# Second layer of a gated attention and expert network on one core: sums of expert rows, norm and rotary attention as one program, loads spread over beats

## What is computed

```python
x = x + tanh(g_xattn[0]) * L0_xattn(_layernorm(x), ctx)   # self-attention with a mask, LN, cross-attention, LN, feed-forward, LN
x = x + tanh(g_ffn[0])   * L0_ffn(_layernorm(x))          # 8 experts, top 2, FF = 1024
x = x + tanh(g_xattn[1]) * L1_xattn(_layernorm(x), ctx, mask)   # rotary cross-attention
x = x + tanh(g_ffn[1])   * L1_ffn(_layernorm(x))          # 8 experts, top 1

# L1_xattn
q = larope(heads(x @ Wq + bq), Lq); k = larope(heads(ctx @ Wk + bk), Lk); v = heads(ctx @ Wv + bv)
scores = where(mask, q @ k.T * 64 ** -0.5, -inf)
return softmax(scores) @ v @ Wo + bo
# L0_ffn
out = out + combine[:, e:e + 1] * (relu(xt @ W1[e] + b1[e]) @ W2[e] + b2[e])   # over the experts e
```

## Time and profile before

| what | value |
| --- | --- |
| median of three runs | 1515.91 us (1514.93 to 1516.16) |
| profiled execution: its time, its span | 1511.45 us, 1509.7 us |
| mean granted clock of PE | 0.917 |
| PE busy in the span | 1216.6 us (81%) |
| DVE / ACT / POOL busy | 749.2 / 565.3 / 419.6 us |
| DMA, mean over the span | 108 GB/s |

### The profile page before, as it was taken

The page is one execution under the profiler, slowest core; times in us unless marked ns, Lnnn a source line. Parts: engine busy times, 40 slices in busy tenths (PEclk is TensorE's granted clock), DMA queues, the critical chain, the costliest instruction groups (busy, mean ns, idle before and its releaser), DMA issues. The chain is left out here.

```text
span 1509.7 us, 27319 instructions
## 1 busy us (share of the span) xinstructions
PE 1216.6 (81%) x8458; PEld 980.7 (65%) x8513; DVE 749.2 (50%) x2742; ACT 565.3 (37%) x1353; POOL 419.6 (28%) x736
## 2 busy tenths in 40 slices
PE   3699989999985999889999996047987865499991
PEld 2466666666653888788888895035665535399991
DVE  3587767676752567743322221846876832122212
ACT  1265656565652322233333332012654541133330
POOL 2434544434334244310000001642334121410004
PEclk9799999999997999999999998567998985699996
DMA  8675676565621920111111112635453204472103
GB/s 216 137 162 149 148 201 151 145 142 147 139 84 52 376 86 36 40 56 36 36 33 35 34 36 90 169 74 106 96 108 72 55 10 153 163 256 90 38 32 118
DMA packets 128612, 162.47 MB, mean 108 GB/s; under 512 B 15444, under 2 KB 113372, under 8 KB 123612
## 3 DMA queue, kind: packets, MB, share of 16 engines
q1 hardware_dynamic: 120072, 133.67, 33.6%
q0 software_dynamic: 8416, 27.27, 5.2%
HBM read 103.23 MB, written 55.19 MB: 105 GB/s over the span
## 5 line engine op out<-in xcount | busy, mean ns | idle before, releaser
L820 DVE CUSTOM_DVE_ANT_0 att_masked_scores<-att_S,Bm 128x256 bf16<-128x256 f32 x512 | 191.6, 419 | 57.4 <-PE att_S L518 46.1
L662 ACT ACTIVATE att_PT<-att_T 128x512 f32<-128x512 f32 x256 | 151.6, 595 | 86.2 <-PE att_T L538 77.1
L1721 ACT ACTIVATE moe_hT<-moe_H,moe_b 128x128 f32<-128x128 f32 x312 | 89.3, 369 | 192.1 <-PE moe_H L1634 191.5
L1987 POOL DMA_INDIRECT comb_g<-yd,dest x48 | 45.7, 952 | 407.1 <-PEq L1971 391.9
L1634 PEld LDWEIGHTS moe_H<-moe_aT,ff_w 128*128 128x128 f32 x1248 | 145.1, 192 | 8.8 <-DVE ff_w L1919 6.2
L1634 PE MATMUL moe_H<-moe_aT,ff_w 128*128 128x128 f32 x1248 | 146.1, 275 | 5.5 <-DVE ff_w L1919 4.9
L1646 PE MATMUL moe_Z<-moe_W,moe_hT 128*128 x624 | 142.5, 381 | 0.8 <-DVE moe_z L1926 0.8
L1646 PEld LDWEIGHTS moe_Z<-moe_W,moe_hT 128*128 128x128 f32 x624 | 115.4, 190 | 15.5 <-issue 1.2
L518 PE MATMUL att_S<-L_KS,L_QS 96*128 96x256 bf16 x512 | 99.2, 276 | 19.5 <-DMA L_KS<-att_k_dram 10.4
L1926 DVE TENSOR_TENSOR moe_z<-moe_Z,moe_b 128x256 f32<-128x256 f32 x39 | 16.6, 424 | 195.5 <-PE moe_Z L1646 195.5
L538 PE MATMUL att_T<-L_QS,L_KS 99*128 99x256 bf16 x512 | 98.4, 273 | 5.3 <-issue 2.6
(11 more groups left out here) (422 smaller groups left out, 2249.4 us busy)
## 6 DMA issues: line engine op xcount, KB each, us to landing
xd<-zero SPq DMA_DIRECT2D x14, 1280.0 KB
moe_W<-in_L_ffn_W SPq DMA_DIRECT2D x16, 1024.0 KB, 13.4
...
att_q_dram<-att_pq SPq DMA_DIRECT2D x16, 384.0 KB, 4.3
att_k_dram<-att_pk SPq DMA_DIRECT2D x16, 384.0 KB, 2.6
L_QS<-att_q_dram SPq DMA_DIRECT2D x16, 384.0 KB, 4.8
L_KS<-att_k_dram SPq DMA_DIRECT2D x16, 384.0 KB, 7.8
...
```

The source lines that it names most:

```text
L662: nc.scalar.activation(PT[:, h % 8, :], bankT[h % 2][:, :], ACT.Exp).then_inc(exp_done, 1)
L820: ins = nc.vector.tensor_tensor_reduce(masked_scores[:, h % 2, u, :], bankS[h % 2][:, u * SEQ:(u + 1) * SEQ], masks[m // B][0][:, u * SEQ: ...
L1721: ins = nc.scalar.activation(eT[:, s % 2, g * P:(g + 1) * P], bankH[half][:, f * P:(f + 1) * P], ACT.Relu, bias=b1[:, bass.ds(e * NF + g, 1)])
```

## The change

- `prepare` loads only what it uses, and rows 0 and 1. The stack rows, rows 2 to 7 and `OUTER` of layer one are issued by SP in beats -4 to -1 of `att`, the context in beat 1, the weights of layer two (ten loads) in beat 2 (`load_in_beats`).
- In `TASKS` and in all engines' loops, rows are turned (and copied by ACT) at head 10 and the output product is made (and added by DVE) at head 12; before it was the other way round.
- `combine` in front of the rotary attention is gone, and `attention_pipeline` has lost its rotary branches. `rotary_pipeline` does both: POOL issues four gathers of 128 expert rows per sequence (`gather`), DVE adds them (`sum_experts`, `sum_rows`) and makes the moments, POOL the roots (`input_roots`, in place of ACT's square root), DVE the norm (`input_norm`).
- In it, keys and values of sequences 0 and 1 are made ahead of the beats, before the first rows are normed; the beats start at -3. SP waits for the spread of queries and of keys by semaphores of their own. V is filled with ones by DVE, not by POOL.
- The instructions of one head, one projection, one split into parts are the same as before.

```diff
@@ prepare, sync
-            rows(0)
+            load_rows(sp, mem, X, a["x"], 0)
...
-            rows(1)
-            load_stack_rows(sp, mem, a["c_stack_rows"])
-            for n in range(2, B):
-                rows(n)
-            load_weights(sp, mem, 0, OUTER)
-            load_weights(sp, mem, 1, INNER + OUTER)
-            load_context(sp, mem)
+            load_rows(sp, mem, X, a["x"], 1)
@@
-         10: (("z", -1),), 11: (("o", 1),), 12: (("x", 4),), 14: (("c", 4),), 15: (("o", 2),)}
+         10: (("x", 4),), 11: (("o", 1),), 12: (("z", -1),), 14: (("c", 4),), 15: (("o", 2),)}
@@
+def load_in_beats(sp, mem, X, x, stack_rows, b):
+    if b == -4:
+        load_stack_rows(sp, mem, stack_rows)
+        load_rows(sp, mem, X, x, 2)
+    if -4 <= b < -1:
+        load_rows(sp, mem, X, x, b + 7)
+    if b == -2:
+        load_rows(sp, mem, X, x, 6)
+        load_weights(sp, mem, 0, OUTER)
+    if b == -1:
+        load_rows(sp, mem, X, x, 7)
+    if b == 1:
+        load_context(sp, mem)
+    if b == 2:
+        load_weights(sp, mem, 1, INNER + OUTER)
@@ attention_pipeline, sync
                     max_to_queries(b + 1)
...
+                load_in_beats(sp, mem, X, *loads, b)
@@ attention_pipeline, tensor (scalar and vector alike)
-                    if h == 10 and has(b - 1):
+                    if h == 10 and has(b + 4):
+                        turn_rows(b + 4)
+                    if h == 12 and has(b - 1):
                         project_out(b - 1)
-                    if h == 12 and has(b + 4):
-                        turn_rows(b + 4)
@@ rotary_pipeline, sync
+            load_rotary(sp, mem)
+            spread_parts(0, 1)
+            stack(0, 1)
+            for b in BEATS:
+                if 3 <= b + 2 < M:
+                    stack(b + 2, 0)
+                    stack(b + 2, 1)
+                if b == -1:
+                    max_to_queries(0)
+                if has(b + 3):
+                    spread_parts(b + 3, 0)
+                    if b + 3 < 3:
+                        stack(b + 3, 0)
+                if b == -3:
+                    load_rest(sp, mem)
+                    spread_parts(1, 1)
+                    stack(1, 1)
+                if b >= 0 and has(b + 1):
+                    max_to_queries(b + 1)
+                if AHEAD <= b + 3 < M:
+                    spread_parts(b + 3, 1)
+                    if b + 3 < 3:
+                        stack(b + 3, 1)
@@ rotary_pipeline, tensor
+            for m in range(AHEAD):
+                turn_context(m)
+                keys(m)
+                project_values(m)
+            turn_rows(0)
@@ rotary_pipeline, scalar
+            bring_context(0)
+            first_part(0, 1)
+            second_part(0, 1)
+            bring_context(1)
+            bring_rows(0)
@@ rotary_pipeline, gpsimd
+            gather(0)
+            gather(1)
+            input_roots(0)
+            parts(0, 1)
+            for b in BEATS:
+                if has(b + 4) and b != -2:
+                    input_roots(b + 4)
+                if has(b + 3):
+                    parts(b + 3, 0)
+                if b == -2:
+                    input_roots(2)
+                if has(b - 2):
+                    inverse_roots(nc, pool, t, moments, root_step, b - 2).then_inc(rooted, 1)
+                if b == -3:
+                    gather(2)
+                    parts(1, 1)
+                if AHEAD <= b + 3 < M:
+                    parts(b + 3, 1)
+                if has(b + 6):
+                    gather(b + 6)
@@ rotary_pipeline, vector
+            def sum_experts(n, i):
+                dve.wait_ge(gathered[n % RING], 16 * NU * TOP * (n // RING + 1))
+                for u in range(NU):
+                    at = n * NU + u
+                    if i:
+                        dve.wait_ge(summed, NU * (TOP * n + 1))
+                    nc.vector.scalar_tensor_tensor(X[:, at, :], g[:, n % RING, i, u, :], weight[i][:, at:at + 1], X[:, at, :],
+                                                   ALU.mult, ALU.add).then_inc(summed, 1)
...
+            nc.vector.memset(V[:, :, :, :], 1.0).then_inc(ready0, 1)
+            dve.wait_ge(mem["k_in"], 16 * 4)
+            turned_keys(0)
+            dve.wait_ge(mem["v_in"], 16 * 3)
...
+            value_rows(0)
+            sum_rows(0)
+            input_moments(0)
+            sum_rows(1)
+            input_norm(0)
+            input_moments(1)
+            turned_keys(1)
+            value_rows(1)
...
+                    if h == 1 and b == -2:
+                        sum_rows(2)
+                        input_moments(2)
+                        sum_rows(3)
+                    if h == (9 if b == -2 else 2) and has(b + 4):
+                        input_norm(b + 4)
...
+                    if h == 5 and b >= -1 and has(b + 5):
+                        sum_experts(b + 5, 0)
+                    if h == 6 and b >= -1 and has(b + 5):
+                        sum_experts(b + 5, 1)
...
+                    if h == 14 and b >= -2 and has(b + 5):
+                        input_moments(b + 5)
@@ flamingo
-            combine(nc, "comb0", X, Y, 2, yd0, dest, weight, mem=mem, stack_rows=a["c_stack_rows"])
-            attention_pipeline(nc, "out", c, mem, X, Y, lambda m: True, gate=gate_x1)
+            rotary_pipeline(nc, "out", c, mem, X, Y, gate_x1, yd0, dest, weight)
```

730 lines of the change are left out of this document (560 added, 170 removed).

## The result

| what | before | changed |
| --- | --- | --- |
| median, beside one another on one chip | 1515.42 us | 1488.91 us (1487.47 to 1490.82) |
| ratio, 95% interval | | 0.9831 [0.9809, 0.9853] |
| span of the profiled execution | 1509.7 us | 1486.2 us |
| mean granted clock of PE | 0.917 | 0.915 |

What follows compares the result with a forecast made beforehand. PE was taken to set the pace in attention, with nobody working between stages. Terms -9.0 - 17.2 + 1.5 - 13.1 + 7.6 gave -30.2 us: 1481.3 us profiled, 1485.7 us against the median, range 1475 to 1501.

Steps and rivals of the forecast that it cites:

- A: Kernel start: loads taken out of the preparation let the first attention start earlier; -9.0 us, bounds -10 and -6.5.
- B: First attention's beats: rows turned at head 10, output product at head 12, so PE's wait goes; -17.2 us.
- Rival 2: First attention: the add at head 12 still waits for `ybb`, all of B is lost; 1502.9 us, chance 0.15.
- C: First attention: loads moved into its beats lengthen them; +1.5 us, bounds 0 and +5.
- D: Rotary start: sums, norm and first keys inside the rotary program bring transposed scores earlier; -13.1 us, bounds -18 and -4.
- Rival 3: Rotary start: held by POOL's queue, so D gives 4 us instead of 13; 1494.8 us, chance 0.1.
- Rival 4: Rotary start: D better than its sum, loads landing at 945 and added DVE work finding gaps; 1478 us, chance 0.1.
- E: Rotary beats 0 to 3: added sums, moments and norms, and late data in beat 0; +7.6 us, bounds +3 and +12.
- Rival 1: Rotary beats -1 to 2: DVE and POOL block one another at sums and norm; 14.4 us, 1500.1 us, chance 0.15.
- Rival 5: Rotary beats -1 to 2: idle gaps drop PE to its lower clock; four such beats give 1570 us, chance 0.02.

Runs made afterwards that it cites:

- experiment 1: Kernel before with only rows turned at head 10 and output product at head 12, in both attention programs: 1494.44 us against 1513.73, ratio 0.9868.
- experiment 2: Kernel before with only the loads moved out of the preparation into the beats: 1512.5 us, ratio 0.9985 to the kernel before.
- experiment 4: Changed kernel with the 1.28 MB fills of zeros taken out of beats 1 and 2 and appended at the end: 1480.71 us, ratio 0.9782.
- experiment 9: Changed kernel with the sums of sequence 3 at head 10 of beat -2, behind the norm of sequence 2: 1491.44 us, ratio 0.9847.
- experiment 5: Changed kernel with the rows of maxima of sequence 0 issued behind the spreads of sequence 2 in rotary beat -1: 1481.47 us, ratio 0.9816.
- experiment 10: Changed kernel without expert-row gathers and sums in the rotary program: its start takes 80.0 us against 95.9, beat 0 27.8 against 27.0.
- experiment 3: Changed kernel with the head exchange undone and the loads back in `prepare`, so the merged rotary program alone: 1505.31 us, ratio 0.9952.
- experiment 6: Changed kernel with POOL's roots behind the parts of the keys and DVE's norm at head 13 in rotary beats: 1472.76 us, ratio 0.9744.

## Why the prediction was right, and where it was not

**A: right.** -9.5 for the start was -10.0, and 0.5 given back in the fill was 1.3: -8.7 at the first exponents against -9.0.

**B: right, with little to spare.** The exchange alone gave 17.1 us in the trace for 17.2, in part by balance: beats 2 to 11 gave 15.0 (1.6 each, not 1.4, but 0.7 in beat 5), beats 12 and 13 1.7 and 1.3, and beat 0 took back 0.9. All or nothing hung on POOL having `ybb` done when the product ends; I gave it 0.5 us of room, and there was none: it ends 0.04 us behind, since the product comes 0.6 us sooner in the beat than worked out. Rival 2 is refuted by experiment 1.

**C: wrong by size, outside its bounds.** +1.5 with bounds 0 and +5; it was 5.4 + 2.7 = 8.1 in beats 2 and 3. The step that failed is "the context costs the same at most, since that beat is not longer". I priced the load by the beat in which it is issued, and that beat (23.70 us) is indeed not longer. The price falls in the next one, where the stack stands behind it; in the beat behind the feed-forward weights it stood there too, and I read it as 1.1 us of that load and not as a stack that had just about come in time. Experiments 2 and 4 show it: with loads alone nearly all of A is gone (2.3 us are left, not told from zero), and without the fills beside them beats 2 and 3 are 1.4 longer, about what I had forecast for C. The Trainium skill, DMA: Bandwidth & Descriptors, section on queues, rings and completion order, says that on each DMA engine descriptors are consumed in ring order; by that rule a small urgent transfer waits for the bytes issued ahead of it. The trace agrees: the last piece of the keys takes 12.0 us to land behind 3.3 MB, and 9.1 behind the fill alone (experiment 1). The rule says nothing of the other part, SP's issues of 3.46 us. Why 2 MB of context held the keys 12.0 us, and 2 MB of feed-forward weights with the same fill 9.0 us one time (PE then waited 1.6), was not tried.

**D: the mechanism right, the size 6.6 us too small.** One step failed and one is open. All of PE's products in the fill were taken at the low clock ("keys and values of sequence 1 are 7.1", "queries 3.4"): they took 3.50 and 1.89, and 1.97, since the clock had come back in between. That and a second context brought 1.6 us sooner put the gather of sequence 3 and the norm of sequence 2 about 4 us earlier than worked out (67.9 instead of 71.5 us after the first gather). The rest, some 3 us, lies behind that norm, where I had put 3 us of DVE work on the path; it is no clear miss, since that stretch takes 27.3 us here and up to 29.9 in kernels of the same order, for 30.3 worked out. Rival 3 had its cause right and its price wrong: POOL's queue does set the norm of sequence 2 (experiment 9), which was in the working, and the start is at 95. Rival 4's better D came, but not by its first cause, loads at 945: the last of them, the key mask, landed 11.6 us after the first gather, 947.8 on the forecast's clock, as worked out. Whether the added DVE work found gaps, its second cause, was not tried.

**E: near for beats 1 to 3, beat 0 forecast at less than half.** Forecast +3.5, +2.5, +1.3, +0.3, measured +8.2, +1.8, +1.3, -0.9. The step that failed is "those scores find their data some 1 to 3 us late". I saw the order of SP, and did not go through its queue to the end: the spread of the queries waits from 1003.3 to 1013.4 for the rows of maxima, the spread of the keys waits for the stack of the queries, and the keys' stack is issued at 1023.8. Experiment 5 takes 4.4 us off beat 0 by the order alone, and experiment 10 shows that with this order it is as long without any sum. The 3.8 us that stay in experiment 5 over the 18.84 of before are near my 3.5; 1 to 2 of them may come with the exchange (experiments 1 and 3), the rest was not taken apart. That the wait for roots in beats 2 to 4 stays as it is was right; experiment 6 prices it at 13 us.

**Rival 1: the mechanism is real, its price small.** Two sums beside POOL's addition for the keys, which had begun 0.12 us ahead of them, take 1.82; beside its gathers 0.86. The Trainium skill, SBUF — State Buffer, section on the two separate sides, calls the port pair that DVE and GpSimd share an exclusive lock, held for the whole instruction by whichever starts first; the trace agrees. The sums read two tensors, the case of the rule that the forecast named; the norm of the earlier trace rows reads one, and two columns. But moved away, the sums cost DVE 4.2 us less over 32 of them and not 14.4, and where it lies on the path (beat 1) 1.4 us. **Rival 5** did not come: the beats keep clocks of 0.87 to 1.00.

So the range held and the centre was 3 us off, in part since errors of opposite sign met: C and E, 6.6 and 3.9 dearer (E from exponents to exponents is 11.5), D 6.6 better at the transposed scores and 8 at the exponents.
